# Differential softmax attention on one core: the two score sets moved to separate halves of the partitions, and the row-maximum units issued in pairs

## What is computed

```
q1, k1, q2, k2, v = split(x_normalised @ Wqkv)        # 16 heads, q and k 8 wide, v 16 wide
A1 = causal_softmax(q1 @ k1.T / sqrt(8)) @ v          # score set 0
A2 = causal_softmax(q2 @ k2.T / sqrt(8)) @ v          # score set 1
diff = A1 - lam * A2                                  # then an RMS norm, and @ Wproj
```

## Time and profile before

| what | value |
|---|---|
| median of three runs | 1667.61 us |
| the profiled execution | 1672.15 us, of which the span is 1670.3 us |
| engines busy over the span | PE 90%, DVE 76%, ACT 66%, POOL 65% |
| heads stage | from about 65 us to about 590 us of the span |
| costliest group | line 610, the exponentials: 576 times 0.600 us |
| second | line 515, the maxima: 640 times 0.628 us |

### The profile page before, as it was taken

How to read it: one execution, slowest core, us unless ns; L and a number is a source line. 1 busy time by engine, 2 the same in 40 slices (tenths; PEclk the granted TensorE clock), 3 DMA queues, 4 the chain that set the end, 5 groups by cost and what they waited for, 6 DMA issues and landing times. The chain is left out here.

```text
span 1670.3 us, 26603 instructions
## 1 busy us (share of the span) xinstructions
PE 1495.2 (90%) x8478; PEld 1012.7 (61%) x8540; DVE 1264.9 (76%) x3430; ACT 1108.1 (66%) x2384; POOL 1087.1 (65%) x1281
## 2 busy tenths in 40 slices
PE   7899999999999767987748999999999999987998
PEld 4334434434434236756646888878888888776675
DVE  5688788888888239642659999999999999873433
ACT  2146666666766737122238999999999999994332
POOL 6205566566565572131448999999999999963353
PEclk9779999999999979999979999999999999999999
DMA  5301001001000033821000000000000100000000
GB/s 202 114 21 39 21 21 39 21 21 40 21 22 20 2 129 109 318 101 51 0 1 1 1 1 1 1 1 1 1 1 1 51 1 1 1 1 1 1 26 26
DMA packets 39812, 59.84 MB, mean 36 GB/s; under 512 B 9132, under 2 KB 33592, under 8 KB 38776
## 3 DMA queue, kind: packets, MB, share of 16 engines
q1 hardware_dynamic: 39528, 56.03, 10.0%
q10 hardware_dynamic: 144, 2.10, 0.3%
HBM read 40.93 MB, written 16.78 MB: 35 GB/s over the span
## 5 line engine op out<-in xcount | busy, mean ns | idle before, releaser
L610 ACT ACTIVATE a_PT<-a_sc 128x512 f32<-128x512 f32 x576 | 317.7, 600 | 187.7 <-PE a_sc L678 128.4
L515 DVE TENSOR_REDUCE a_mpart<-a_nat 128x1 f32<-128x512 f32 (+3 forms) x640 | 364.3, 628 | 78.1 <-PE a_nat L645 41.0
L2057 DVE BATCH_NORM_STATS2 c_stat<-c_R 128x6 f32<-128x512 f32 x576 | 381.3, 680 | 2.0 <-ACT c_R L1976 2.0
L2021 POOL TENSOR_SCALAR c_R<-big,c_negtau 128x256 f32<-128x256 f32 x264 | 300.7, 1164 | 32.1 <-DVE c_negtau L2090 27.1
L2021 POOL TENSOR_SCALAR c_R<-c_Z,c_negtau 128x256 f32<-128x256 f32 x255 | 290.5, 1165 | 19.7 <-DVE c_negtau L2123 18.7
L642 PE MATMUL a_nat<-mem 96*128 96x512 bf16 (+3 forms) x768 | 243.6, 345 | 21.1 <-DVE a_mpart L515 10.9
L1893 PE MATMUL c_z<-mem,c_R 128*128 128x256 f32 x1024 | 231.9, 380 | 0.0
L482 POOL TENSOR_SCALAR_AFFINE_SELECT a_PT<-a_PT 128x512 f32<-128x512 f32 x128 | 79.0, 636 | 221.6 <-ACT a_PT L610 221.6
L1976 ACT ACTIVATE c_R<-c_Z,c_negtau 128x256 f32<-128x256 f32 x513 | 215.6, 513 | 0.4 <-DVE c_negtau L2123 0.4
L1976 ACT ACTIVATE c_R<-big,c_negtau 128x256 f32<-128x256 f32 x504 | 212.5, 514 | 3.1 <-DVE c_negtau L2090 1.7
L1893 PEld LDWEIGHTS c_z<-mem,c_R 128*128 128x128 f32 x1024 | 193.4, 190 | 25.6
(11 more groups left out here) (316 smaller groups left out, 2470.5 us busy)
## 6 DMA issues: line engine op xcount, KB each, us to landing
mem<-qk_parts SPq DMA_DIRECT2D x360, 32.0 KB
qk_parts<-a_parts SPq DMA_DIRECT2D x16, 384.0 KB, 2.6
made<-f_made SPq DMA_DIRECT2D x24, 256.0 KB, 2.8
mem<-made SPq DMA_DIRECT2D x3, 2048.0 KB, 7.8
X<-in_L_attn_x_dram SPq DMA_DIRECT2D x4, 512.0 KB, 6.9
mem<-in_L_ffn_wq_dram SPq DMA_DIRECT2D x1, 2048.0 KB, 14.9
ternary<-f_W_T ACTq DMA_DIRECT2D x1, 2048.0 KB, 8.3
mem<-in_L_ffn_wo_dram SPq DMA_DIRECT2D x1, 2048.0 KB, 14.1
```

Of the source, the lines that this page charges most:

```text
L515: dve.tensor_reduce(mpart[:, b, j:j + cnt, i, k0 // 512], src, AX.X, ALU.max).then_inc(s_max, 1)
L610: act.activation(PT[:, n % 3, c, :], sc[:, u % 2, :], ACT.Exp, scale=SCALE0).then_inc(s_exp, 1)
L2021: pool.tensor_scalar(split(i, h) if r < NR else whole(i, h), scores_of(i)[:, h, :], threshold(i, r, h), 0.0, ALU.add, ALU.max).then_inc(s_ ...
L2057: dve.bn_stats(stat[:, r, b, :], R[:, slot(i), b, :]).then_inc(s_stat, 1)
```

## The change

Set 0 now lies in partitions 0 to 63 and set 1 in partitions 64 to 127 of `QS` and `KS`: 48 rows of parts, then three rows for the maxima (`QS`) against ones (`KS`). Both tiles are half as long in the free dimension. Every score matmul uses rows of one half only, 48 for a natural unit and 51 for a score product. Units are issued in pairs, one of each set, the matmuls of the two in turn. The mask is added in two steps, since each set has only 64 rows: once with its own half of the identity and the mask, once with copies whose halves are swapped (four new transfers). The narrow units join two diagonal places of one set instead of one place of both. The number of units (40 a head), their widths and the maxima are as before. The score products of a chunk go in the order `SET_ORDER`, so that the sets alternate. A pair stands between the first and the second product of each half of a chunk, and where before there were two units at four places, there are now two pairs at two places. One memset of 3072 columns replaces the three of 6144.

The core of the diff (the index changes that follow from the new layout are left out):

```diff
-STK = 6 * HD0
-MROW = 96
+STK, SIDE = 6 * HD0, 64
...
+    shapes = [[(i, 0, 512)] for i in range(3, TB)] + [[(7, 512, 512)], [(2, 0, 384)], [(6, 512, 384)],
+                                                      [(1, 0, 256), (5, 512, 256)], [(0, 0, 128), (4, 512, 128)]]
+    return [(j, segs) for segs in shapes for j in (1, 0)]
+SET_ORDER = (0, 2, 1, 3)
...
+            sp.wait_ge(s_ident, 3)
+            for whole, swapped in ((K.ident_bf, K.ident_swap), (K.mask, K.mask_swap)):
+                for half in range(2):
+                    sp.dma_start(swapped[SIDE * half:SIDE * half + SIDE, :],
+                                 whole[SIDE * (1 - half):SIDE * (2 - half), :]).then_inc(s_swap, 16)
...
-                    sp.wait_ge(s_zero, 3)
+                    sp.wait_ge(s_zero, 1)
                     load_head(sp, K, 0, 0, slice(0, T), K.s_first)
...
-            pool.memset(K.QS[:].bitcast(F32), 0.0).then_inc(s_zero, 1)
+            pool.memset(K.KS[:].bitcast(F32), BF16_ONES).then_inc(s_zero, 1)
...
-            pool.memset(K.KS[0:MROW].bitcast(F32), 0.0).then_inc(s_zero, 1)
...
-            pool.memset(K.KS[MROW:P].bitcast(F32), BF16_ONES).then_inc(s_zero, 1)
...
+            def unit_pair(h, u):
...
+                if NU * h.n + u > 2:
                     pe.wait_ge(s_max, h.count(NU, u - 2))
+                if NU * h.n + u + 1 > 2:
+                    pe.wait_ge(s_max, h.count(NU, u - 1))
+                pair = [units[u], units[u + 1]]
+                for n in range(len(pair[0][2])):
+                    for e, (b, j, segs) in enumerate(pair):
+                        (i, k0, w), rows = segs[n], slice(SIDE * j, SIDE * j + STK)
+                        q, out = b * T + i * P, nat[:, (NU * h.k + u + e) % 3, n * w:(n + 1) * w]
+                        ins = pe.matmul(out, QS[rows, h.buf, q:q + P], KS[rows, h.buf, b * T + k0:b * T + k0 + w],
+                                        start=True, stop=i * P - k0 >= w)
+                        if n == len(segs) - 1 and i * P - k0 >= w:
+                            ins.then_inc(s_nat, 1)
+                    for half, (unit, mask) in enumerate(((K.ident_bf, K.mask), (K.ident_swap, K.mask_swap))):
+                        for e, (b, j, segs) in enumerate(pair):
+                            (i, k0, w), side = segs[n], slice(SIDE * j, SIDE * j + SIDE)
+                            diag = i * P - k0
+                            if diag < w:
+                                out = nat[:, (NU * h.k + u + e) % 3, n * w + diag:n * w + diag + P]
+                                ins = pe.matmul(out, unit[side, :], mask[side, :], start=False, stop=half == 1)
...
-                    for c in range(4):
+                    for c in (0, 2):
                         scores(h, n, c)
-                        k = 4 * n + c
-                        for _ in range(NU * (k + 1) // (4 * NCH) - NU * k // (4 * NCH)):
+                        k = 2 * n + c // 2
+                        for _ in range(NU // 2 * (k + 1) // (2 * NCH) - NU // 2 * k // (2 * NCH)):
                             next(between, None)
-                        if c == 1:
+                        scores(h, n, c + 1)
+                        if c == 0:
```

More of the change, by code:

```diff
@@ L359, in attention_heads @@
     qk_parts, VA = K.qk_parts, K.VA
-    units = [(b, n) + u for b in range(2) for n, u in enumerate(max_units())]
+    units = [(b,) + u for b in range(2) for u in max_units()]
     NU, NCH = len(units), len(PROB_CHUNKS)
@@ L419, in maxima @@
                     for part in range(3):
-                        sp.dma_start(QS[MROW + part:MROW + part + 1, h.buf, j, :].rearrange("a (r q) -> a r q", q=P),
+                        row = SIDE * j + STK + part
+                        sp.dma_start(QS[row:row + 1, h.buf, :].rearrange("a (r q) -> a r q", q=P),
                                      msplit[16 * j:16 * j + 16, part, :]).then_inc(s_mld, 16)
@@ L507, in unit_maxima @@
             def unit_maxima(h, u):
-                b, _, segs, cnt = units[u]
+                b, j, segs = units[u]
                 dve.wait_ge(s_nat, h.count(NU, u + 1))
@@ L633, in unit_scores @@
                     pe.wait_ge(s_load[h.buf], 16 * HEAD_LOADS * (h.times + 1))
-                if not isinstance(h.n, int) or NU * h.n + u > 2:
+                if NU * h.n + u > 2:
                     pe.wait_ge(s_max, h.count(NU, u - 2))
-                b, _, segs, cnt = units[u]
-                for s, (j, i, k0, w) in enumerate(segs):
-                    out = nat[:, (NU * h.k + u) % 3, s * w:(s + 1) * w]
-                    q = b * T + i * P
-                    diag = i * P - k0
-                    ins = pe.matmul(out, QS[0:MROW, h.buf, j, q:q + P], KS[0:MROW, h.buf, j, b * T + k0:b * T + k0 + w],
-                                    start=True, stop=diag >= w)
-                    if diag < w:
-                        ins = pe.matmul(out[:, diag:diag + P], K.ident_bf[:], K.mask[:], start=False, stop=True)
-                ins.then_inc(s_nat, 1)
+                if NU * h.n + u + 1 > 2:
[16 more added lines that the diff above has]
+                                ins = pe.matmul(out, unit[side, :], mask[side, :], start=False, stop=half == 1)
+                                if n == len(segs) - 1 and half == 1:
+                                    ins.then_inc(s_nat, 1)
             def turn_max(h):
@@ L659, in maxima @@
                     return
-                for u in range(FIRST, NU):
-                    unit_scores(first, u)
+                for u in range(FIRST, NU, 2):
+                    unit_pair(first, u)
                     yield
-                for u in range(FIRST):
+                for u in range(0, FIRST, 2):
                     if u == GAP or not second.exists():
@@ L667, in maxima @@
                             return
-                    unit_scores(second, u)
+                    unit_pair(second, u)
                     yield
@@ L677, in scores @@
                 for kt, q0, w in PROB_CHUNKS[n]:
-                    ins = pe.matmul(sc[:, u % 2, col:col + w], KS[:, h.buf, j, b * T + kt * P:b * T + (kt + 1) * P],
-                                    QS[:, h.buf, j, b * T + q0:b * T + q0 + w], start=True, stop=True)
+                    ins = pe.matmul(sc[:, u % 2, col:col + w], KS[rows, h.buf, b * T + kt * P:b * T + (kt + 1) * P],
+                                    QS[rows, h.buf, b * T + q0:b * T + q0 + w], start=True, stop=True)
                     col += w
@@ L736, in period @@
                     pass
-            for u in range(FIRST):
-                unit_scores(Head(0, 0), u)
+            for u in range(0, FIRST, 2):
+                unit_pair(Head(0, 0), u)
             for _ in maxima(Head(0, -1)):
@@ L755, in alloc_attention @@
     flat = K.mem3[:].rearrange("p a n -> p (a n)")
-    half = 3 * B * T
-    K.QS, K.KS = (flat[:, e * half:(e + 1) * half].bitcast(BF16).rearrange("p (b j t) -> p b j t", b=3, j=2) for e in range(2))
+    half = 3 * B * T // 2
+    K.QS, K.KS = (flat[:, e * half:(e + 1) * half].bitcast(BF16).rearrange("p (b t) -> p b t", b=3) for e in range(2))
+    K.ident_swap, K.mask_swap = (flat[:, 2 * half + e * P // 2:2 * half + (e + 1) * P // 2].bitcast(BF16) for e in range(2))
     K.rms = sb("rms", [P, NT, H0])
```

37 lines of the change are left out of this document (12 added, 25 removed).

## The result

The median with the change is 1718.2 us (1715.7 to 1724.64, four runs) against 1668.03 us (1667.5 to 1671.32, four runs on the same chip): a ratio of 1.0296, 95% interval 1.0282 to 1.0310. It is slower by 50 us, where 9 were forecast, and outside the range. The profiled execution took 1719.13 us with a span of 1717.4, which is 47.1 more than before.

The account below looks back on a forecast made before the run. A loop through PE and ACT was taken to set the pace, with DVE next. Input stage -3.9, prologue +8 and heads +4.8 gave +8.9 us, a median of 1676.5 us, range 1648 to 1700.

Parts of the forecast that it names:

- What bounds the kernel: Steady heads: a loop through PE and ACT sets the pace, 3.11 us a plain chunk; DVE is the next limit.
- The halves side by side: Score matmuls on PE: the two row halves run together, so a pair costs PE what one unit did.
- The input stage: Before the first reduction: one shorter memset frees the queue of head loads before the last stores, -3.9 us, between 0 and -5.
- The prologue: Before the heads, PE at half clock: pairs run ahead by less, leaving gaps on DVE, +8 us, bounds 0 and 12.
- The head: Walk through a head's nine chunks: 31.42 us against 31.10, times 15 heads +4.8 us.
- 3-4: Chunk 3 to 4, two pairs in a row with three buffers: 4.05 us, before 3.35, a loss of 0.70.
- 8-0: Chunk 8 to 0 of the next head, a chain of three pairs: 4.02 us, before 3.45, a loss of 0.57.
- 6-7: Chunk 6 to 7, where DVE splits the maxima: 3.58 us, before 4.03, one unit fewer ahead of the value block.
- 4-5: Chunk 4 to 5, where the narrow pair waits for DVE: 3.21 us against 3.18.
- The gain of five chunks: Time saved in five of a head's chunks, 1.07 us, used up by two double-pair places (1.27) and small change.
- slower by the clock: Second rival: PE streams less and its granted clock falls, 105 us over the heads, near 1780 us; chance 0.06.
- The sum: Whole kernel: -3.9 + 8 + 4.8 = +8.9 us on the profiled 1672.15, that is 1681; median 1676.5.

Follow-up runs that it names:

- own waits: Changed kernel in its order, but each unit waits singly for the unit three before it, matmuls of one unit after the other: 1667.68 us, one execution.
- the old layout with pairs: Against the changed kernel: 96-row units, 128-row products, one mask matmul and the earlier input stage, keeping its pairs, waits and places: 1739.67 us, ratio 1.0420.
- the one of 1660 us: Changed kernel with single waits per unit, plus unread products of the other half beside those of the last head, begun two chunks earlier: 1660.06 us, ratio 0.9942.
- the two with filler in the last head and in the prologue: Changed kernel with unread matmuls added, beside each last-head product (1710.40 us) or, in the other run, two behind every prologue pair (1717.14 us).
- doubled units in the middle heads: Changed kernel with every unit's score matmuls issued twice into the same place in heads 2 to 15: 1759.13 us, one execution.

## Why the prediction was wrong

- **What bounds the kernel**: right. PE lost 4.3 us of busy time a head and nothing came of it; the loop through PE and ACT, and the units' waits for DVE, set the pace.
- **The halves side by side**: right (384 columns twice in 0.34 us).
- **The input stage** (-3.9): measured -5.0, the end of my bounds. The mechanism holds, but part of the size is scatter: over the eleven kernels with halves the first reduction starts between 60.8 and 62.4 us.
- **The prologue** (+8): measured +7.3, by the mechanism given, a pair that must find two buffers free. With own waits it was 22.97, before 22.46. The 8 itself is a little rough: the gaps that I list for ten pairs add up to about 2.7, not 2.9.
- **The head** (+0.32 forecast, +1.40 measured): this step failed in size. The failing terms are "a pair waits for the unit two before its first one and starts 0.06 later" and the reductions behind it. The pair has two wait instructions in a row, and starts 0.146 later; one of them gone gave back 0.5 to 0.8 a head. And I counted reductions by their distance in a row (0.46 to 0.50 for 384 columns). A wait sees the end of the last one, its own length: 0.557 for 384 columns (the mean of 546 ns stands in the earlier trace rows). At 3-4 the first pair goes 1.54 after the third product and not 1.41, the second 1.17 after the first and not 1.06, which is 0.24 of the 0.26. Both errors occur only where PE waits, so they fell on 3-4, 8-0, 6-7 and 4-5, and the rest of the walk held. Of the three parts of a pair that the runs told apart, I had seen the common wait, half seen the turns, and missed the doubled wait. (The gain of five chunks, which I gave as 1.07, comes to 0.97 by my own terms; the sum of 31.42 is right.)
- **The rival "slower by the clock"**: this is the other failed step, 0.06 given to it and taken as all or nothing. It came in parts: 13.7 us in the middle heads, 8.4 in the last, 6.9 in the first (8.2 less the 1.4 of every head: the clock rose at 117.5 instead of 101.4, and dipped once more). Part of the 6.9 belongs to the pairs: in the old layout with pairs the clock rose at 118.0, and by the same sum 3.1 were lost. After the heads 5.1 came back, which leaves 23.9. That part is not the layout's, since the old layout with the pairs takes 1075.3 there as well: half of it falls in the first 10 us behind the last exponential, half more than 500 us later, and how much of it is the clock was not worked out. I had taken the last head of before, 7.08 of 10 us in flight at 1.00, as evidence that the clock holds. Busy time does not show how many rows are in use, and the layout that halves them is what changed: no kernel with the old layout (before, and two experiments) had the lower clock in the heads after the first, ten of the eleven with halves had it, all but the one of 1660 us. The last head takes 38.2 to 38.9 in the three with the old layout, 45.2 to 49.7 in the eight with halves and no filler there, and 38.1, 41.2 and 43.4 in the three with it.
- **The Trainium skill** ("TensorE: Matmul & The Clock Gate", A second HAM failure mode: psum-queue depth-cycling) tells also of a kernel whose TensorE idles for moments between groups of matmuls while it cycles through PSUM buffers, and whose clock goes back and forth. That is nearer to this case than the long gaps I had weighed it by. The trace agrees that it goes back and forth, with gaps of up to 0.76 us on PE in the heads at the full clock, but the old layout has such gaps too (up to 0.96 in the last head of before) and stays at 1.00.
- **The sum**: against +8.9 on the profiled execution, +47.1 were measured. The heads' waits are 16.2 of the 38.2 missed (15 x 1.08), the clock and what came back behind the heads 23.9, the first two stages -1.8. I can't say which head the clock falls in: three executions that run the same code in heads 2 to 15 (the change and the two with filler in the last head and in the prologue) took 14.5, 6.2 and 6.3 us more than 14 x 32.50 there, which is some of the scatter of 1715.7 to 1724.6.

Open: what about the half rows brings the clock down. Filler in the other half of the last head helped (38.1, 41.2 and 43.4 instead of 46.6), though it held the clock throughout only once; doubled units in the middle heads and filler in the prologue did not. In the middle heads the places and waits matter too: with halves and the change's places, but the matmuls of one unit after the other (own waits, or a common wait), none after the first had the lower clock, and so own waits alone took away nearly all of the 50 us (1667.68, one execution). Why is open as well. The number of rows itself, with all else the same, was not varied.

## What to carry to other kernels

A group that waits as one for several buffers costs more than its parts that wait singly, even when it makes the work itself cheaper: with three buffers, and one wait instruction too many, it turned a gain of 0.6 us a head into a loss of 1.4, and units of different halves overlap with their neighbours without being grouped. Count every wait instruction on the waited path, and take the full length of what is waited for, not its pace in a row. When a change uses fewer rows of TensorE, look at the granted clock of every stretch, not at the busy share.

## What I had not expected of the hardware

- A second wait ahead of a matmul, met already, adds 0.09 us (146 ns over 131 pairs against 57 ns over 116).
- In the last head of the change, 46.6 us with products over 51 rows, the clock is at 0.50 for 30 us; with products over 128 rows it stays at 1.00. The time in flight, which is itself longer at the lower clock, is not less with 51 rows: 24.69 of 33 us for 128 rows, 34.40 of 42 for 51 (with own waits).
- A product over one half and a unit over the other, with nothing but their order to bring them together, start 0.01 us apart.
